# An attention and mixture-of-experts kernel: GpSimd's scaling of the attention outputs is held until the fourth step's masks of a later group

## The reference

```python
q = x @ Wq;  k, v = split(concat(mem, x) @ Wkv)
dots = q @ k.T * scale;  dots[j > i + mem_len] = -inf
out = softmax(dots) @ v;  x = x + out @ Wout + bout
```

## Time and profile before

| | |
|---|---|
| time, median of 3 runs | 375.83 us (374.93 to 376.63) |
| the profiled execution's own time | 376.98 us |
| its span, first to last instruction | 375.2 us |
| TensorE busy | 352.5 us, 94% |
| ScalarE busy | 266.3 us, 71% |
| VectorE busy | 211.8 us, 56% |
| GpSimd busy | 117.9 us, 31% |
| mean granted TensorE clock | 0.971 of full |

### The profile page before, as it was taken

How to read it: one execution, slowest core, us unless ns; L and a number is a source line. 1 busy time by engine, 2 the same in 40 slices (tenths; PEclk the granted TensorE clock), 3 DMA queues, 4 the chain that set the end, 5 groups by cost and what they waited for, 6 DMA issues and landing times.

```text
span 375.2 us, 10982 instructions
## 1 busy us (share of the span) xinstructions
PE 352.5 (94%) x4336; PEld 228.0 (61%) x4336; DVE 211.8 (56%) x724; ACT 266.3 (71%) x385; POOL 117.9 (31%) x178
## 2 busy tenths in 40 slices
PE   8999999899999999999999999996858999999993
PEld 7757547343544444443534445585747899999992
DVE  4999698353637455563737445398778332323231
ACT  2675563899999999999999999614871545454630
POOL 5445775000004030300304030601431646464522
PEclk9999999899999999999999999999795999999999
DMA  7733799500538435553449513800660522322100
GB/s 245 199 111 116 247 238 312 183 6 3 140 108 271 122 101 139 155 140 96 119 130 260 126 36 63 279 0 2 224 226 3 146 88 65 106 73 92 59 26 31
DMA packets 37325, 47.68 MB, mean 127 GB/s; under 512 B 8764, under 2 KB 26610, under 8 KB 37265
## 3 DMA queue, kind: packets, MB, share of 16 engines
q1 hardware_dynamic: 34368, 40.26, 36.8%
q0 software_dynamic: 2560, 6.30, 5.6%
q10 hardware_dynamic: 337, 0.32, 0.3%
HBM read 32.71 MB, written 13.81 MB: 124 GB/s over the span
## 4 chain that ended last, share of the span: by engine, by line
PE 76%; DVE 10%; ACT 9%; issue 2%; POOL 2%; POOLq 0%
PE ps L1116 18%; PE ps L1092 16%; PE ps L1297 10%; PE ps L1309 9%; PE ps L1077 8%; ACT pbuf L858 8%; PE ps L1029 5%; DVE pbuf L1632 4%; PE ps L1230 3%; PE ps L999 1%; DVE stats L1666 1%; DVE xe L1661 1%; PE ps L1286 1%; PE ps L1178 1%; POOL pbuf L754 1%
## 5 line engine op out<-in xcount | busy, mean ns | idle before, releaser
L858 ACT ACTIVATE pbuf<-ps 128x1024 f32<-128x1024 f32 (+3 forms) x192 | 169.4, 1028 | 3.2 <-PE ps L1092 3.0
L1632 DVE SCALAR_TENSOR_TENSOR pbuf<-pbuf,seen 128x128 f32<-128x128 f32 (+2 forms) x288 | 76.4, 307 | 65.5 <-ACT pbuf L858 64.5
L1092 PE MATMUL ps<-q_st,k_st 98*32 98x512 bf16 (+4 forms) x2048 | 102.0, 319 | 2.8 <-ACT pbuf L858 2.6
L1116 PE MATMUL ps<-pbuf,v_st 128*32 128x512 f32 (+4 forms) x1024 | 98.0, 478 | 1.9 <-DVE pbuf L1632 1.9
L1092 PEld LDWEIGHTS ps<-q_st,k_st 98*32 98x32 bf16 x2048 | 51.8, 96 | 69.8 <-issue 28.1
L726 POOL TENSOR_TENSOR mid<-mid 64x256 f32<-64x256 f32 x28 | 20.5, 763 | 120.9 <-DMA mid<-reciprocals 120.9
L1116 PEld LDWEIGHTS ps<-pbuf,v_st 128*32 128x32 f32 x1024 | 27.5, 110 | 26.9 <-issue 11.8
L1297 PEld LDWEIGHTS ps<-mid,piece_f 128*128 128x128 f32 x320 | 38.7, 192 | 1.6 <-issue 0.7
L1297 PE MATMUL ps<-mid,piece_f 128*128 128x128 f32 x320 | 39.0, 275 | 0.5 <-issue 0.5
L1309 PE MATMUL ps<-pbuf,mid 128*128 128x256 f32 x160 | 37.7, 380 | 0.0
L940 ACT ACTIVATE mid<-ps 128x512 f32<-128x512 f32 x20 | 11.9, 597 | 34.4 <-PE ps L1297 34.3
(11 more groups left out here) (253 smaller groups left out, 370.2 us busy)
## 6 DMA issues: line engine op xcount, KB each, us to landing
wts<-in_L_ffn_W SPq DMA_DIRECT2D x16, 512.0 KB, 5.0
k_st<-k_cut SPq DMA_DIRECT2D x48, 147.2 KB, 3.0
q_st<-q_cut SPq DMA_DIRECT2D x48, 128.0 KB, 2.9
q_cut<-wts SPq DMA_DIRECT2D x8, 384.0 KB, 3.4
k_cut<-wts SPq DMA_DIRECT2D x8, 384.0 KB, 3.9
token_rows<-xe SPq DMA_DIRECT2D x4, 512.0 KB, 4.2
mid<-mid SPq DMA_DIRECT2D x28, 64.0 KB, 2.6
mid<-reciprocals SPq DMA_DIRECT2D x28, 64.0 KB, 2.3
```

The source lines that it names most:

```text
L858: nc.scalar.activation(pbuf[:, s % 2, r, c0:c1], st_ps[(s * GH + r) % NST][:, c0:c1], ACT.Exp, scale=SCALE).then_inc(exp_done, 1)
L1092: last = nc.tensor.matmul(st_ps[(s * GH + r) % NST][c:c + 32, a:z], k_st[pa][:, r, t * P + c:t * P + c + 32], q_st[pa][:, r, q0 + a - c0:q ...
L1116: last = nc.tensor.matmul(o_ps[32 * r:32 * r + 32, a:z], v_st[pa][:, t, r, :], pbuf[:, s % 2, r, a + dc:z + dc], start=(t == 0), stop=(t = ...
L1632: last = nc.vector.scalar_tensor_tensor(a, a, 3.0e38, seen[:, off:off + w], ALU.min, ALU.mult)
```

## The change

`scale(g)` gets one more wait: for g up to 5 it also waits for the masks of group g + 2 through its fourth step (step 3, `NARROW - 1`). In the loop it is called one turn later, as `scale(g - 1)` behind the `load_v` of group g + 2, and the last one, `scale(6)`, behind the loop. The wait for `v_in` is raised by one to fit the new order. Nothing else changes.

```diff
+NARROW = STEP_TILES.index([1])
...
             def scale(g):
...
-                pool.wait_ge(v_in, min(g + 3, 2 * NG))
+                pool.wait_ge(v_in, min(g + 4, 2 * NG))
                 pool.wait_ge(packed, 16 * GH * (g + 1))
                 pool.wait_ge(den_in, 16 * GH * (g + 1))
+                if g + 2 < 2 * NG:
+                    pool.wait_ge(mask_done, (g + 2) * ((NSTEP - 1) * GH) + (NARROW - 1) * GH)
...
                 if g + 2 < 2 * NG:
                     pool.wait_ge(pv_done, (g + 1) * NSTEP + 2)
                     load_v(g % 2, (g + 2) // NG, (g + 2) % NG // 2)
-                scale(g)
+                if g > 0:
+                    scale(g - 1)
+            scale(2 * NG - 2)
```

## The result

Timed side by side, the changed kernel took 374.30 us (median of 14 runs, 373.67 to 375.32) and the kernel before 376.32 us (14 runs, 374.56 to 378.00). The ratio is 0.9957 with a 95% interval of 0.9945 to 0.9970, so 1.6 us less, with 1.1 to 2.1 in the interval. The forecast was 1.9 us. The profiled execution has a span of 372.3 us against 375.2.

What follows compares the result with a forecast made beforehand. The prediction took ScalarE's exponentials and TensorE's work as the floor, with values waiting for VectorE's masks behind GpSimd's scaling. -2.09 + 0.2 gave -1.9 us: 375.83 to 373.9 us, 8 in 10 from 372.9 to 376.2.

Steps and rivals of the forecast that it cites:

- The floor and the sum: Groups 1 to 6: ScalarE's exponentials and TensorE's work set 21.07 us; four groups exceed it by 2.09 us in all.
- Removing the scaling from the start: Start of groups 2 to 7: four scaling instructions fewer each, gaining 2.09 us, between 0 and 4.1 us.
- The move of `load_v`: Group start: `load_v` goes ahead of the scaling, over at 92.10 before the first mask; cost nothing.
- Step 4 as the new place: Scaling in step 4 of the same group ends just before the fourth mask; costs 0.03 us a group, 0.2 in all.
- Rival C: Step 4: fourth mask waits for the whole fourth scaling instruction in every group; slower, 378.1 us at the full 0.73; chance 0.09.
- Rival B: Step 4: scaling ends 0.1 to 0.4 us too late for the fourth mask, giving 1.5 us back; 375.2 us; chance 0.18.
- The median: Whole execution: the profiled execution's 1.9 us taken from the median of the runs, 375.83 us, giving 373.9 us.
- rival D: Group starts: the loss is rarely there without the profiler, or staging becomes the next wait; 375.0 to 375.9 us; chance 0.15.
- A: The forecast itself: group starts fall to the floor and step 4 hides the scaling; 373.9 us, 372.8 to 374.6; chance 0.58.
- Staging and the waits for `scaled`: Staging transfers and those waiting for `scaled`, spreading and output projection: cost nothing; staging 1 us if one in three came late.

Runs made afterwards that it cites:

- the run with one column: Kernel before with each scaling instruction cut to one column, outputs otherwise left unscaled; 400.97 us, with changed expert-layer work, groups at 21.06 to 21.07 us.
- the eight shorter instructions: Kernel before with the scaling cut into 8 instructions of 128 columns a group in place of 4 of 256; 377.07 us, ratio 1.0009.
- the order alone: Changed kernel without its new wait for masks: `load_v` goes ahead and the scaling follows once its reciprocals have landed; 376.14 us, ratio 0.9991.
- the pair at 1.4 us: Changed kernel with the scaling released by VectorE's copy, copy to `v_st` ahead (377.69 us, ratio 1.0028) or behind (380.03 us, ratio 1.0097).
- the wait alone: Kernel before with only the new wait for the fourth step's masks, the loop's old order kept; 375.77 us, ratio 0.9972.
- copy late: Kernel before with the copy to `v_st` held until the same group's fourth step's masks are done, scaling at its old place; 375.78 us, ratio 0.9969.

## Why the prediction was right, and where it was not

**The floor and the sum** held. The prediction took 2.09 us from four groups of one trace; the profiled pair shows 2.05, every group is at 21.07, and the run with one column shows that no place for the scaling gives less.

**Removing the scaling from the start** was right in size for that trace, but the cause was drawn too narrowly. The prediction read the masks' 0.75 us as each mask letting one scaling instruction pass; the eight shorter instructions, with masks 0.47 us apart, bear that out. But it gave the loss to the scaling alone, and the order alone brought five groups to 21.09 to 21.24 us with the scaling still on the masks. What sets the loss is how late GpSimd lets go of the burst: scaling and copy are one stretch of 3.8 us in the kernel before. The prediction also took 0.68 us as the worst place; 1.35 us into the group cost 0.90 in the second trace. And it listed the loss against the start for groups 2, 4 and 5 only: group 6, at 1.15 us, lost the same 0.68 as group 2 at 0.98.

**The move of `load_v`** was costed at nothing, with group 1 as the witness. Nothing is right as a cost: 0.72 us, over before the first mask. That it could be a gain was missed; the pair at 1.4 us puts it at 0.52 us a group where the copy stood behind the scaling. In the whole change this is hidden, since the wait alone also reaches 21.07.

**Step 4 as the new place** held to a tenth: an end 0.09 to 0.18 us ahead of the last mask was forecast, 0.02 to 0.04 is measured, since the scaling begins 0.17 us after step 3's last mask (123.51, to 123.68) and not 0.09. The cost was taken as 0.03 us a group, 0.2 in all, and is at most 0.06 us in all six. Rival C did not come, but its mechanism did when it was asked for: 0.60 us later the scaling costs 0.41 us a group. Rival B, some 0.25 us a group, has nothing in the trace.

**The median** was forecast 1.9 us down by taking the profiled execution's loss for every one. That is the term whose size was off. The second trace of the kernel before loses 1.31 us against the changed kernel in groups 1 to 6, and 0.18 more in group 7 (the statistics behind it begin at 22.34 us in place of 22.16), so rival D was in part true beside A. And the 0.23 us outside the span, which no sum of groups shows, was not in the sum at all: with it the first trace promises 1.8 us and the second 1.3, and the measured 1.6 lies between them. That the two medians lie 2.0 us apart, next to the forecast's 1.9, is luck: the changed kernel timed again gained 0.5 us at its ratio of 0.9986, the wait alone, with the same groups, 1.1. The size of the gain in a whole execution is therefore known to no better than about 1 us; that of the groups is known to tenths in each trace.

**Staging and the waits for `scaled`**: no wait for a transfer to `q_st` or `k_st` shows in the changed kernel; its longest group, the fifth with 21.12 us, is 0.05 over the floor, and in the second trace no group is. And the last two scalings run back to back (5.93 us from 229.07) and end at 235.00; the projection's tiles that need them come behind 243.69 us (L1183).

## What to carry to other kernels

When a background job on GpSimd shares memory with VectorE's masks, lay the whole stretch that it occupies, helpers behind it included, against the times at which the consumer needs the last mask, and ask what each late end costs; cutting it into shorter instructions lengthened the stretch and did not lower the sum of the groups here. A job that starts when a DMA happens to land costs a different amount in each execution, and a wait on an event of the pipeline pins it, but a good place can end 0.04 us from its edge: run it 0.6 us later once, to know. And take the size of a gain from two traces of the kernel before, not from one.

## What the runs showed of the hardware

VectorE's copy out of PSUM took 1.22 to 1.23 us beside GpSimd's copy (changed kernel, 111.64), beside its scaling (kernel before, 134.16) and with GpSimd idle (scaling at VectorE's copy with the copy to `v_st` behind, 134.09), while step 4's masks, with both inputs in SBUF, went from 0.27 to as much as 0.70 us. That is as the Trainium skill has it (SBUF — State Buffer, section Who interferes with whom): a VectorE instruction with at most one SBUF input, outside its 2-port modes, does not contend with GpSimd. GpSimd's own stretch hardly grows beside dense masks: 2.81 us nearly alone, 3.05 us beside the twelve masks of step 3; the waiting is nearly all VectorE's there. It is not always so: the last scaling of the kernel before took 3.19 us beside masks that kept their 0.29.

Two executions of one kernel differ by more than this change: the fourteen of the kernel before spread over 3.4 us. Windows that end at group 1's start, of the kernel before and of the changed kernel:

```profile
60.00:91.34 31.34, 29.88 (x452) 14.27 (x454) 14.26 (x58) 26.14 (x32) 3.73 (x5) 0.95 0.31 106
```

```profile
60.00:90.57 30.57, 29.11 (x457) 14.71 (x459) 15.12 (x59) 26.77 (x33) 4.58 (x5) 1.00 0.33 108
```

In the first the granted clock is 0.95 over the window, in the second 1.00. Windows of the kernel before in group 0, 4 us in which TensorE pauses and what comes behind them:

```profile
66.00:70.00 4.00, 2.80 (x56) 0.96 (x52) 0.97 (x3) 4.00 (x5) 0.00 (x0) 1.00 0.19 44
70.00:73.60 3.60, 3.60 (x40) 1.06 (x31) 1.48 (x6) 2.85 (x4) 0.00 (x0) 0.53 1.00 370
```

The clock stands at the lower of its two levels until some 73.6 us. In the changed kernel TensorE was busy for the same 2.80 of 4 us (67 to 71 us), and in the windows 67 to 71 and 71 to 75 us the clock is 1.00: it did not fall. Of the fourteen traces of this study seven have the fall (0.94 or 0.95 in the first window), both of the kernel before among them, both of the changed kernel not. From its first scores to the start of group 1, group 0 takes 26.13 to 26.22 us in the seven and 24.60 or 24.61 in the others, so the fall costs 1.6 us. The seven began group 0 earlier, at 64.75 to 65.26 us against 65.40 to 66.03, which leaves 0.9 us of it at group 1's start and covers the 0.77 us. Kernels with the scaling at its old place fall on both sides (one column and eight instructions without the fall, copy late and the kernel before with it), and the scaling does not run yet in group 0; whether the kernel before is more prone to it than the changed one, two traces of each can't say.

And behind group 6 the changed kernel took 155.3 us in its first trace and 157.3 in its second, in code that the change doesn't touch. ScalarE's copy ahead of the first expert matmuls, and these matmuls, in the first and in the second trace:

```profile
291.16 0.37 ACT L940 COPY mid<-ps 128x256 f32<-128x256 f32 x1 [3.23 <-PE ps L1291]
291.63 1.13 PE L1302 MATMUL ps<-mid,piece_f 128*128 128x128 f32 x8 [0.51 <-issue]
```

```profile
292.40 0.37 ACT L940 COPY mid<-ps 128x256 f32<-128x256 f32 x1 [5.01 <-remote]
292.87 1.13 PE L1302 MATMUL ps<-mid,piece_f 128*128 128x128 f32 x8 [2.07 <-issue]
```

The granted clock of the 5 us from 70 us behind the start of group 7 is 1.00 in one (287.03 to 292.03) and 0.74 in the other (286.47 to 291.47), but the clock is the smaller part: the transposes ahead (L1291) begin 73.70 and 73.95 us after the start of group 7, 0.25 apart, and L1302 74.60 and 76.40, 1.8 apart. ScalarE's copy between them comes late in the second trace, 1.59 us behind the transposes in place of 0.04; what held it no trace names. The kernel before had a granted clock of 0.80 in these 5 us and took 155.35 us, no longer than the changed kernel's first trace. In the eleven other traces whose expert layer has the same work the time behind group 6 lies between 155.3 and 158.1 us. That scatter is as large as the change, and can account for ratios of 0.9957, 0.9972 and 0.9986 for kernels with the same groups.
